# K and Q laid out as head pairs, a new order in the scan on every engine, and a spread second group norm

## What is computed

```python
x = x + conv3x3(relu(gn(x) * mask(gn(x)))) + bias      # mask from each channel's centre of mass
x = x + ttt(gn(x))                                     # 784 tokens of 128 channels per image

# ttt: q, k, v of 8 heads x 16 dims, rope on q and k; then a scan over 49 chunks of 16 tokens
def step(carry, inp):
    W1c, b1c = carry
    xq, xk, xv, et = inp
    Z1 = xk @ W1c + b1c
    grad = ln_l2_bwd(Z1, xv - xk, g, bb)
    Attn1 = tril(xq @ xk.swapaxes(-1, -2))
    b1_bar = b1c - tril(et) @ grad
    Z1_bar = xq @ W1c - et * Attn1 @ grad + b1_bar
    W1n = W1c - (last_eta * xk).swapaxes(-1, -2) @ grad
    b1n = b1c - (last_eta * grad).sum(-2, keepdims=True)
    return (W1n, b1n), xq + ln(Z1_bar, g, bb)
# then layer norm over 128 channels and the output projection
```

## Time and profile before

| | |
|---|---|
| median of 3 runs | 1983.95 us (1970.23 to 1985.82) |
| the profiled execution | 1980.83 us |
| its span in the profile | 1979.0 us |
| mean granted PE clock, share of 2.4 GHz | 0.638 |
| busy share of the span: PE, PEld, DVE, ACT, POOL | 82, 61, 77, 51, 67% |
| instructions | 82050 |
| transfers | 148.82 MB in 1650519 packets, 1630176 of them under 512 bytes |

### The profile page before, as it was taken

The page is one execution under the profiler, slowest core; times in us unless marked ns, Lnnn a source line. Parts: engine busy times, 40 slices in busy tenths (PEclk is TensorE's granted clock), DMA queues, the critical chain, the costliest instruction groups (busy, mean ns, idle before and its releaser), DMA issues.

```text
span 1979.0 us, 82050 instructions
## 1 busy us (share of the span) xinstructions
PE 1626.2 (82%) x33524; PEld 1208.9 (61%) x33524; DVE 1518.3 (77%) x3567; ACT 1017.6 (51%) x2487; POOL 1316.5 (67%) x1480
## 2 busy tenths in 40 slices
PE   4778898903888888988988888889889888888886
PEld 2444454501776766766766767767667666666674
DVE  6987766604888878888888888888888887888864
ACT  3434656542555555555555555555555555555543
POOL 2263535474778777777777777777777777777753
PEclk9899999955556555556565655555655666555555
DMA  6077698963457566666665665665666665656554
GB/s 239 1 39 60 99 85 69 81 165 46 61 69 80 67 71 75 71 74 71 72 77 69 74 76 66 75 78 68 74 73 73 74 73 68 77 66 75 66 60 49
DMA packets 1650519, 148.82 MB, mean 75 GB/s; under 512 B 1630176, under 2 KB 1643744, under 8 KB 1650144
## 3 DMA queue, kind: packets, MB, share of 16 engines
q1 hardware_dynamic: 1390640, 117.87, 51.1%
q10 hardware_dynamic: 259504, 25.70, 10.8%
HBM read 40.71 MB, written 38.54 MB: 40 GB/s over the span
## 4 chain that ended last, share of the span: by engine, by line
SPq 23%; PE 17%; DVE 16%; DMA 9%; issue 8%; ACT 3%; DVEq 0%; POOL 0%; ACTq 0%; POOLq 0%
SPq L479 16%; DMA kqk<-work 8%; SPq L495 6%; PE p_kt L1641 6%; PE p_x L1685 4%; DVE work L1315 2%; DVE work L1282 2%; DVE work L1306 2%; PE p_m L1670 2%; DVE work L1375 1%; PE p_x L1676 1%; DMA late<-work 1%; DVE zs L1362 1%; DVE m L1369 1%; DVE work L1397 1%
## 5 line engine op out<-in xcount | busy, mean ns | idle before, releaser
L816 ACT ACTIVATE work<-p_kt 128x512 f16<-128x512 f32 x196 | 148.2, 756 | 215.3 <-PE p_kt L1641 215.2
L1641 PEld LDWEIGHTS p_kt<-fold,kqk 128*128 128x128 f16 x6272 | 184.9, 104 | 98.4 <-ACT work L816 47.2
L1641 PE MATMUL p_kt<-fold,kqk 128*128 128x16 f16 x6272 | 201.1, 175 | 53.0 <-DMA kqk<-work 43.6
L1614 PE MATMUL p_j<-wa,work 128*128 128x512 f16 x196 | 119.5, 610 | 148.0 <-DVE work L1282 103.0
L626 POOL TENSOR_TENSOR work<-work,rope_s 128x256 f32<-128x256 f32 x196 | 160.9, 841 | 85.5 <-DVE work L1282 85.5
L597 POOL TENSOR_TENSOR work<-work,g 128x256 f32<-128x256 f32 x98 | 71.7, 732 | 206.0 <-DVE work L1353 203.2
L1544 PE MATMUL p_j<-work 128*128 128x392 f16 x864 | 158.5, 344 | 30.7 <-POOL work L540 18.3
L1315 DVE TENSOR_TENSOR work<-work 128x256 f16<-128x256 f32 x196 | 162.0, 880 | 15.8 <-ACT work L803 15.8
L1685 PEld LDWEIGHTS p_y<-w,late 128*128 128x128 f16 x4704 | 146.6, 104 | 19.6 <-issue 9.7
L1685 PEld LDWEIGHTS p_x<-w,late 128*128 128x128 f16 x4704 | 148.9, 105 | 12.3
L1614 PEld LDWEIGHTS p_j<-wa,work 128*128 128x128 f16 x196 | 24.9, 127 | 208.3 <-issue 177.4
(11 more groups left out here) (174 smaller groups left out, 4438.5 us busy)
## 6 DMA issues: line engine op xcount, KB each, us to landing
kqk<-work SPq DMA_DIRECT2D x392, 64.0 KB, 4.7
late<-work SPq DMA_DIRECT2D x392, 64.0 KB, 3.7
late<-work SPq DMA_DIRECT2D x392, 32.0 KB, 2.5
out_y<-work ACTq DMA_DIRECT2D x49, 256.0 KB, 6.8
x_scratch<-late SPq DMA_DIRECT2D x24, 392.0 KB, 11.7
xs_scratch<-work SPq DMA_DIRECT2D x24, 392.0 KB, 6.5
work<-x_scratch ACTq DMA_DIRECT2D x49, 192.0 KB, 3.7
work<-xs_scratch SPq DMA_DIRECT2D x48, 192.0 KB, 2.9
```

The lines of the kernel that those rows point to most:

```text
L816: return act.activation(kqt16[:, o, g:g + GP, :, :, :].rearrange("p g h t a -> p g a (h t)"), p_kt[:, :].rearrange("p (g a n) -> p g a n", ...
L1614: pe.matmul(p_j[k][:, 0:4 * C], tokens(s, k, 0), wa16[:, :], start=True, stop=False, skip_group_check=True)
L1641: mm = pe.matmul(p_kt[:, at:at + CS], part_of(g + k, h, a), fold16[:, :], start=True, stop=True)
```

## The change

K and Q go into `hl16` as head pairs: for each partition the order is now (pair of heads, dimension, half, head of the pair) where it was (head, dimension, half). So a piece of the K/Q transfer that lies in one run holds two heads, 128 bytes instead of 64, and there are half as many; the bytes are the same. In the blocks that PE reads as weights the columns of one head lie 4 fp16 elements apart (8 bytes) instead of 2. The `turn` lists of SP, POOL, ACT, DVE and PE get new orders. In the convolution stage the second group norm is spread over two images: the mean is taken after the second half of image 1 of the group, the variance, root and scaling at image 2, and `scaled_at` starts one image later.

Indentation is cut by 8 in the diff.

```diff
@@ -20,6 +20,7 @@
 NG = B // GB
 NCH = HW // CS
 GP = 2
+HP = NH // 2
 NS = NCH * GP
 SC = GP * C
 ROWS = 14
@@ -166,9 +167,9 @@
 ktqt0 = second.cut([2, NG, NH, GB, CS, 2], F16)
 ktqt = [ktqt0, ktqt1]
 third = 4 * NH * GB * 2 * HD
-kq_sets = [kqk[:, 0:2 * third].rearrange("p (s b e) -> p s b e", b=GB, e=2 * HD),
-           kqk[:, third:3 * third].rearrange("p (s b e) -> p s b e", b=GB, e=2 * HD)]
-blocks = kqk[:, :].rearrange("p (o g h b d a) -> p o g h b d a", o=3, g=NG, h=NH, b=GB, a=2)
+kq_sets = [kqk[:, 0:2 * third].rearrange("p (s b e) -> p s b e", b=GB, e=4 * HD),
+           kqk[:, third:3 * third].rearrange("p (s b e) -> p s b e", b=GB, e=4 * HD)]
+blocks = kqk[:, :].rearrange("p (o s b d a j) -> p o s b d a j", o=3, s=NG * HP, b=GB, a=2, j=2)
 k_of = [0, 2]
 tables = Carver(kqk[:, :].bitcast(F32))
@@ -212,7 +213,7 @@
 scan = Carver(work)
 xs_in = scan.cut([2, B, CS, 2], F16)
-hl16 = scan.cut([2, 2, NG, C, 2], F16)
+hl16 = scan.cut([2, 2, NG * HP, HD, 2, 2], F16)
 nrm = scan.cut([3, SC])
 ra = scan.cut([2, SC])
 rb = scan.cut([2, SC])
@@ -369,6 +370,12 @@
 def over_pair(ap):
     return ap.rearrange("p (o c) -> p o c", o=1).to_broadcast([128, GP, C])
+def split(ap):
+    return ap.rearrange("p (s j d) -> p s j d", j=2, d=HD)
+def half_of(c, at, g, a):
+    return hl16[:, c % 2, at, g * HP:(g + GP) * HP, :, a, :].rearrange("p s d j -> p s j d")
 def pair(ap):
     return ap.rearrange("p (g c) -> p g c", g=GP)
@@ -380,10 +387,10 @@
 def scaled_at(b):
-    q, i = (b - 2) // GB - 1, (b - 2) % GB
-    if q < 0 or i > 5:
+    q, i = (b - 3) // GB - 1, (b - 3) % GB
+    if q < 0 or i > 4:
         return []
-    return [GB * q + k for k in ([i] if i < 4 else [4 + 2 * (i - 4), 5 + 2 * (i - 4)])]
+    return [GB * q + k for k in ([i] if i < 2 else [2 * i - 2, 2 * i - 1])]
 @block.sync
@@ -473,7 +480,7 @@
             sp.wait_ge(fold_q_done.sem, fold_q_done.count(2 * c - 1))
         if c >= 2:
             sp.wait_ge(grad_done.sem, grad_done.count(2 * c - 3))
-        part = hl16[:, c % 2, :, :, :, :].rearrange("p o g (h d) a -> p (o g h) (d a)", d=HD)
+        part = hl16[:, c % 2, :, :, :, :, :].rearrange("p o s d a j -> p (o s) (d a j)")
         for b in range(GB):
             at = slice(b * CS, (b + 1) * CS)
             sp.dma_start(kq_sets[c % 2][at, :, b, :], part[at]).then_inc(kq_landed.sem(c), 16)
@@ -509,10 +516,10 @@
             sp.dma_start(whole[at, :, b, :], part[at]).then_inc(m_landed.sem(c), 16)
     def turn(k):
-        kq_spread(k - 3)
         m_spread(k - 4)
+        turned_spread(k - 3)
+        kq_spread(k - 2)
         xs_next(k)
-        turned_spread(k - 3)
     for k in range(NCH + 4):
         turn(k)
@@ -658,32 +665,32 @@
         pool.tensor_tensor(u[:, s % 4, :], u[:, s % 4, :], nrm[:, 2, :], ALU.subtract).then_inc(target_done.sem, 1)
     def turn(k):
+        b_low(2 * k - 7)
+        rope_sum(2 * k - 2)
+        w_low(2 * k - 7)
+        g_scaled(2 * k - 6)
+        g_hat(2 * k - 6)
+        g_dot(2 * k - 6)
+        k_scaled(2 * k - 2)
+        q_out(2 * k - 2)
+        target(2 * k - 2)
+        g_both(2 * k - 6)
+        g_scaled(2 * k - 5)
         g_hat(2 * k - 5)
         g_dot(2 * k - 5)
+        o_scaled(2 * k - 7)
         rope_sin(2 * k - 1)
-        o_scaled(2 * k - 7)
+        o_sum_q(2 * k - 7)
         g_both(2 * k - 5)
         rope_sum(2 * k - 1)
         k_scaled(2 * k - 1)
-        o_sum_q(2 * k - 7)
-        w_low(2 * k - 6)
         target(2 * k - 1)
         q_out(2 * k - 1)
+        w_low(2 * k - 6)
         b_low(2 * k - 6)
+        o_scaled(2 * k - 6)
         rope_sin(2 * k)
-        o_scaled(2 * k - 6)
         o_sum_q(2 * k - 6)
-        rope_sum(2 * k)
-        b_low(2 * k - 5)
-        w_low(2 * k - 5)
-        g_scaled(2 * k - 4)
-        g_hat(2 * k - 4)
-        g_dot(2 * k - 4)
-        k_scaled(2 * k)
-        target(2 * k)
-        q_out(2 * k)
-        g_both(2 * k - 4)
-        g_scaled(2 * k - 3)
     for k in range(NCH + 4):
         turn(k)
@@ -755,6 +762,8 @@
     mask_parts(2)
     for b in range(B):
         i, q = b % GB, b // GB
+        if i == 2 and q > 0:
+            gn_root(2 * q + 1, GB * (q - 1), GB)
         if b + 3 < B:
             if (b + 3) % GB == 0:
                 act.wait_ge(gn_v.sem, gn_v.count("shift", 2 * ((b + 3) // GB)))
@@ -762,8 +771,6 @@
             add_bias(b + 3)
         if i == 4 and q < NG - 1:
             gn_root(2 * q + 2, GB * (q + 1), GB)
-        if i == 1 and q > 0:
-            gn_root(2 * q + 1, GB * (q - 1), GB)
         if b + 2 < B:
             relu(b + 2)
         if b + 3 < B:
@@ -800,7 +807,7 @@
             act.wait_ge(kq_landed.sem(c - 2), kq_landed.count(c - 2))
         for o in range(2):
             at = o if c % 2 == 1 else 1 - o
-            last = act.activation(hl16[:, c % 2, at, g:g + GP, :, 0], pair(qk[:, o, :]), ACT.Copy)
+            last = act.activation(half_of(c, at, g, 0), split(qk[:, o, :]), ACT.Copy)
         last.then_inc(qk_high_done.sem, 1)
     @guard_chunk
@@ -932,40 +939,40 @@
         act.dma_start(xr[:, c % 2, FRONT:B, :], x2_t[:, :, CS * c:CS * (c + 1)].rearrange("b c n -> c b n")).then_inc(xr_landed.sem(c), 16)
     def turn(k):
-        b_high(2 * k - 6)
-        w_high(2 * k - 6)
+        xr_load(k - 4)
+        o_square(2 * k - 7)
+        kt_copy(2 * k - 4)
+        z_square(2 * k - 5)
+        post_root(2 * k - 8)
+        kt_copy(2 * k - 3)
+        z_root(2 * k - 5)
+        post_copy(2 * k - 9)
+        o_root(2 * k - 7)
+        g_high(2 * k - 6)
+        qt_copy(2 * k - 4)
+        post_norm(2 * k - 8)
+        qt_copy(2 * k - 3)
+        y_store(k - 5)
+        rate_gate(k - 2)
         g_high(2 * k - 5)
         qk_high(2 * k - 1)
-        y_store(k - 5)
+        post_copy(2 * k - 8)
         x_square(2 * k)
         o_square(2 * k - 6)
-        post_copy(2 * k - 8)
         ln_root(2 * k)
+        b_high(2 * k - 6)
         post_root(2 * k - 7)
+        w_high(2 * k - 6)
         o_root(2 * k - 6)
         post_norm(2 * k - 7)
+        w_high(2 * k - 5)
         b_high(2 * k - 5)
-        w_high(2 * k - 5)
-        xr_load(k - 3)
         z_square(2 * k - 4)
         z_root(2 * k - 4)
         qk_high(2 * k)
+        x_square(2 * k + 1)
         m_high(k - 2)
-        x_square(2 * k + 1)
-        kt_copy(2 * k - 2)
         ln_root(2 * k + 1)
-        o_square(2 * k - 5)
-        post_root(2 * k - 6)
-        z_square(2 * k - 3)
-        o_root(2 * k - 5)
-        kt_copy(2 * k - 1)
-        z_root(2 * k - 3)
-        post_copy(2 * k - 7)
-        g_high(2 * k - 4)
-        qt_copy(2 * k - 2)
-        post_norm(2 * k - 6)
-        qt_copy(2 * k - 1)
-        rate_gate(k - 1)
     for k in range(NCH + 5):
         turn(k)
@@ -1230,9 +1237,9 @@
             stats_half(d, 1)
         if turn:
             gn_centre(2 * q + 2, GB * (q + 1), GB)
-        if second_turn:
-            gn_centre(2 * q + 1, GB * (q - 1), GB)
         add_conv(b, 0)
+        if i == 2 and q > 0:
+            gn_scale(2 * q + 1, GB * (q - 1), GB)
         if ahead:
             stats_image(d)
         add_conv(b, 1)
@@ -1241,7 +1248,7 @@
         if turn:
             gn_scale(2 * q + 2, GB * (q + 1), GB)
         if second_turn:
-            gn_scale(2 * q + 1, GB * (q - 1), GB)
+            gn_centre(2 * q + 1, GB * (q - 1), GB)
     for b in range(B):
         image(b)
@@ -1312,8 +1319,7 @@
         dve.wait_ge(qk_high_done.sem, qk_high_done.count(s))
         for o in range(2):
             at = o if c % 2 == 1 else 1 - o
-            last = dve.tensor_tensor(hl16[:, c % 2, at, g:g + GP, :, 1], pair(qk[:, o, :]),
-                                     hl16[:, c % 2, at, g:g + GP, :, 0], ALU.subtract)
+            last = dve.tensor_tensor(half_of(c, at, g, 1), split(qk[:, o, :]), half_of(c, at, g, 0), ALU.subtract)
         last.then_inc(qk_low_done.sem, 1)
     @guard_chunk
@@ -1470,57 +1476,57 @@
                                  op0=ALU.add, op1=ALU.add).then_inc(final_done.sem, 1)
     def turn(k):
+        g_along(2 * k - 6)
+        o_sum(2 * k - 7)
+        post_inverse(2 * k - 8)
+        z_sum(2 * k - 5)
+        ln_inverse(2 * k - 1)
+        g_rated(2 * k - 6)
+        z_inverse(2 * k - 5)
+        norm(2 * k - 1)
+        z_hat(2 * k - 5)
+        o_inverse(2 * k - 7)
+        b_step(2 * k - 6)
+        o_hat(2 * k - 7)
+        g_low(2 * k - 6)
+        z_rate(2 * k - 5)
+        final(2 * k - 9)
+        rope_cos(2 * k - 1)
+        g_means(2 * k - 5)
+        g_along(2 * k - 5)
+        g_centre(2 * k - 5)
+        post_stats(2 * k - 7)
+        rate_scaled(k - 1)
+        g_rated(2 * k - 5)
+        w_step(2 * k - 6)
+        g_low(2 * k - 5)
+        qk_low(2 * k - 1)
         post_aggr(2 * k - 7)
         ln_inverse(2 * k)
         norm(2 * k)
         o_sum(2 * k - 6)
         post_inverse(2 * k - 7)
+        b_step(2 * k - 5)
         o_inverse(2 * k - 6)
-        b_step(2 * k - 5)
         o_hat(2 * k - 6)
         w_step(2 * k - 5)
-        final(2 * k - 8)
```

(52 more changed lines are left out.)

## The result

The changed kernel takes 1992.55 us (median of 11 runs, 1989.97 to 1997.14), the one before 1977.15 (11 runs, 1970.23 to 1985.82): ratio 1.0083, 95% interval 1.0064 to 1.0103. It is slower by a little under 1%, where 1932 us was forecast. Of all executions in this document two stand far outside, 2234 us in the run e8 and 3590 us in e15; no ratio uses them.

The account below looks back on a forecast made before the run. The loop through `norm` over PE, ACT and DVE was taken to bound the scan. Turn 30.18 - 0.91 - 0.13 + 0.35 = 29.49 us saves 34 us, group norm 15: 1981 to 1932 us, range 1875 to 1972.

Parts of the forecast that it names:

- The loop and its terms: Scan: the loop through `norm` over PE, ACT and DVE takes 28.91 us; PE waits in it every turn, without slack.
- K/Q transfers: SP, head pairs: eight issues fall from 10.99 to 6.5 us, landing from 4.7 to 3.2; the folds' wait goes whole.
- the 0.91: PE in the scan: the folds' wait for K/Q transfers, 0.91 us a turn, taken off the turn once.
- Reads with the 8-byte step: PE: `fold` and `grad` read K/Q weights 8 bytes apart, 224 loads a turn; extra cost taken as nothing.
- Rival (c): PE weight loads at 8 bytes double: 6.6 us a turn, about 2255 us; slower from 5 ns a load on; chance 0.08.
- Writes of ACT and DVE: Halves written with a step of 8: taken as 0; 0.5 us a turn on DVE would fall into its wait before `norm`.
- Order: New turn lists: `g_rated` 1.0 us later, `y_store` 0.3 off ACT's loop; net +0.7, half taken, +0.35 us a turn.
- The store's new place: `y_store` moves beside the turned blocks, up to 1.5 us more there; half of `z_state`'s wait kept, 0.13 us a turn.
- Group norm: Convolution: waits for sums vanish at images 9, 17, 25; variance waits near 6 us at 10, 18, 26; 15 us saved.
- The sum: Whole kernel: a turn of 29.49 us saves 34 us and the group norm 15, giving 1932 us from 1981.
- a rival of the order: Rival (b): the loop through `norm` takes back all, 1.0 to 1.3 us more; turn 30.0, 1964 us; chance 0.17.
- the same: Whole kernel: outcome within about 1% (20 us) of the kernel before, given 0.15.

Follow-up runs that it names:

- e8: Kernel before, with only the load of the next x (`xs_next`) moved behind K/Q in SP's list: ratio 1.0003 to before.
- e15: Kernel before, with only the load of the residual's x moved to the end of ACT's turn: ratio 0.9888 to before.
- e9: Kernel before, with two ACT moves: store of y behind the next odd step's square, residual's x load at the turn's end: ratio 0.9639 to before.
- e1: Kernel before plus only the head pairs (layout, transfers, 8-byte reads and writes); old turn lists and group norm: ratio 0.9948 to before.
- e4: Kernel before, with only the K/Q weight reads of fold and `grad` at 8 bytes instead of 4 (wrong columns, same work): ratio 1.0136 to before.
- e6: Kernel before plus the new turn lists and 8-byte K/Q weight reads (wrong columns, same work); old layout, transfers and writes: ratio 1.0063 to before.
- e11: Kernel before plus the head pairs, with ACT and DVE writing the two heads of a pair innermost: ratio 0.9942 to before.
- e5: Changed kernel without the head pairs: new turn lists and spread group norm on the old K/Q layout: ratio 0.9870 to before.
- e3: Kernel before plus only the spread second group norm; scan and layout as before: ratio 0.9958 to before.
- e7: Changed kernel, with ACT and DVE writing the two heads of a pair innermost: ratio 0.9986 to before.
- e16: Kernel before plus late y store and x load on ACT, spread group norm, and head pairs written pair innermost: ratio 0.9621 to before.

## Why the prediction was wrong, step by step

**The loop and its terms: right.** 28.91 us without the K/Q wait was the reading; e9 takes most of that wait away and the store's issue out of ACT's part, and has 28.74.

**K/Q transfers: right in size, in part by luck.** In the changed kernel eight issues take 6.22 to 6.63 us (6.5 forecast), one lands in 3.3 (3.2), and the folds' wait is gone. But the pairs alone (e1) land in 4.1 us; it takes the load of x out of their midst to come to 3.3, and that was in no term. The gain in the old order is 38 us where 45 was taken. In the whole change it is only some 9, because the order takes most of the same wait away. The forecast's sum had the 0.91 only once, so this is no error of the total; but the term was put down to the layout, and the layout then had to be worth it, which it is not: in the new order it returns 9 us for its cost.

**Reads with the 8-byte step, taken at 0: the step that failed.** The loads of folds and `grad` are busy 225.4 + 171.4 us for 184.9 + 132.2, 1.63 us a turn, 7.3 ns for each of 224. Of that 0.62 to 0.65 us a turn reaches the time (e4, e6), 1.4 to 1.6%. Rival (c) had the mechanism and a chance of 0.08, at a price (a load doubled) far above what happened, and its turning point of 5 ns a load charged all of PE's extra work to the path; by the runs about 0.4 of it gets there. The inference from two equal rows (steps of 2 and 4 bytes, both 104 ns) to a third was extrapolation over an edge that no row showed. The same holds for the page that I let confirm it: the Trainium skill, SBUF — State Buffer (Door 1), has full bandwidth for two hits in a 16-byte line, by which, as I read it, a step of 8 bytes is free. The loads here took 118 ns for 104, so the measurement speaks against that and decides.

**Writes of ACT and DVE, taken at 0: failed too.** "0.5 us on DVE would fall into its wait ahead of `norm`" was right for the order of before (e11, e1). But ACT was forgotten in the sentence: the two high halves take 1.36 us for 0.81 on the loop, and DVE's low half then waits for them (75.8 us for 15.8). In the new order that is 0.38 us a turn (30.65 against 30.27), 1.0%. A cover read in the old order was used for the new one.

**Order: right in sum, for a reason that is open.** Forecast +0.22 a turn beside the K/Q wait; measured -0.44 with 33.9 / 49 = 0.69 of that wait gone, so +0.25. The stretch from `z_inverse` to `g_rated` was forecast at +1.0 us and is +1.4 (e5). The stretch was to set the time, but most of what came into DVE's stretch can be moved out again and nothing is gained, and by the waits POOL is as late. The store's new place beside the turned blocks did as forecast: `z_state` on PE waits 7.6 us for them in all, 0.16 a turn where 0.13 was kept.

**The store of y and the load of x: the miss that would have been worth most.** I weighed only the store's new place, and not the load's move at all. Their old places cost 3.6% together (e9), of which the load's alone is 1.1% (e15). K/Q landed in 4.7 us where M's took 2.5, with a load of 192 KB issued in their midst, and I put all of the difference down to pieces.

**Group norm: right in kind, 8 to 10 us for 15.** The scan starts 9.9 us earlier; e3 gives 0.42%, 8 us. PE's waits for the last sums of a group, which were to vanish, only fell from 27.3 us in four to 13.4 in three. Those for the variance, which were to be some 6 us at each of the three next images, are 13.4 in all seven (10.6 before). The changed kernel, variance first:

```profile
PE p_out L1540 <- DVE work L1001: 13.4, 7, 4.9
PE p_out L1536 <- DVE work L1093: 13.4, 3, 8.5
```

**The sum.** 29.49 was forecast, 30.65 measured; reads 0.62 and writes 0.38 make 1.00 of the 1.16. The rest is small: without the pairs the new order stands at 29.77 (e5), 0.28 above the forecast, and the transfers give some 0.12 of that back. The slower side of 1% was given 0.09, by (c) alone; the measured 0.8% lies in the 0.15 for the same, but 20 us above the range, whose upper end was set by a rival of the order and by no term for the steps.

## What to carry to other kernels

A layout that makes transfers cheaper must be priced at every reader and writer, above all at the one instruction that runs 224 times a turn; where no row has the new step, its cost is a bound and not zero. Two parts that remove the same wait earn it once and each keep their own cost: run or reason each part on top of the others. And before a transfer is cut into better pieces, look at what else is in flight beside it; moving a load and a store away from it cost two lines here and gave 3.6% (a part of that is the store's issue leaving ACT's part of the loop).

## What the runs showed of the chip

- fp16 weights of 128 x 128 read with a column step of 4 elements (8 bytes): 118 ns a load against 104 at 1 or 2 elements, at the same granted clock (e4 against before); 32 loads and matmuls of a fold stand at 1.22 us in the trace against 1.00.
- An ACT copy of 128 x 256 fp32 to fp16 that writes single elements 8 bytes apart took 823 ns, single ones 4 bytes apart 476, neighbouring pairs 8 bytes apart 463 (it reads its source in the same order as it writes). On DVE the subtraction that makes the low half took 1098, 880 and 881 ns in the old order of instructions (e1, before, e11), and 1079, 815 and 794 in the new (after, e5, e7).
- 64 KB within SBUF in 1024 pieces of 64 bytes landed in 4.7 us beside the load of x, in 3.7 with that load elsewhere (e15) and in 3.6 with the store of y elsewhere too (e9). In 512 pieces of 128 bytes it landed in 4.1 beside the load (e1) and in 3.3 without (e16). So more of what looked like the price of small pieces was another transfer in flight.
